# The second mixture's down product in three f32r passes of high and low parts instead of one f32 product

## The reference, cut to what matters

```
logits = xt @ gate_w.T
_, idx = top_k(logits + beta, 2)
c = zeros.at[..., idx].add(sigmoid(logits[idx]))
g = einsum('bh,ehm->bem', xt, gate_proj_w)
u = einsum('bh,ehm->bem', xt, up_proj_w)
h = silu(g) * u
eo = einsum('bem,emh->beh', h, down_proj_w)
combined = einsum('beh,be->bh', eo, c)
... shared_out: the same with the shared weights, without c
x = x + combined + shared_out
```

## Time and profile before

| | |
|---|---|
| median of 3 runs | 2351.04 us (2350.42 to 2353.8) |
| the profiled execution | 2356.89 us |
| its span, first to last instruction | 2355.1 us |
| mean granted TensorE clock over the span | 0.921 |
| TensorE busy | 2025.9 us (86%), weight loads 1358.8 us |
| VectorE, ScalarE, GpSimd busy | 981.7, 1002.4, 674.1 us |
| one expert of the second mixture in the chain | 17.83 us, nine of them |

### The profile page before, as it was taken

The page is one execution under the profiler, slowest core; times in us unless marked ns, Lnnn a source line. Parts: engine busy times, 40 slices in busy tenths (PEclk is TensorE's granted clock), DMA queues, the critical chain, the costliest instruction groups (busy, mean ns, idle before and its releaser), DMA issues. The chain is left out here.

```text
span 2355.1 us, 35383 instructions
## 1 busy us (share of the span) xinstructions
PE 2025.9 (86%) x13548; PEld 1358.8 (58%) x13548; DVE 981.7 (42%) x1616; ACT 1002.4 (43%) x1352; POOL 674.1 (29%) x322
## 2 busy tenths in 40 slices
PE   6599999899978999999998676767898989688899
PEld 2475656656556566665665354436644944356787
DVE  2365454554617545556461244325300700355222
ACT  1144444444434444444443032114798689432321
POOL 1015554454660645445556003001000000000221
PEclk9799999999989999999999588788899989888899
DMA  5200000000021000000000400002454346200121
GB/s 178 61 21 6 5 15 1 15 5 1 1 55 49 6 1 15 5 15 5 1 1 4 121 0 0 1 29 63 75 97 82 76 78 108 73 1 1 54 80 62
DMA packets 81637, 86.43 MB, mean 37 GB/s; under 512 B 29865, under 2 KB 71537, under 8 KB 78161
## 3 DMA queue, kind: packets, MB, share of 16 engines
q1 hardware_dynamic: 74312, 81.35, 14.3%
q10 hardware_dynamic: 7176, 2.94, 0.5%
HBM read 54.38 MB, written 4.72 MB: 25 GB/s over the span
## 5 line engine op out<-in xcount | busy, mean ns | idle before, releaser
L727 POOL TENSOR_TENSOR sums<-sums,probs 128x1024 f32<-128x1024 f32 x224 | 532.9, 2379 | 322.8 <-ACT probs L765 286.8
L819 DVE TENSOR_REDUCE part_max<-psum_banks 128x2 f32<-128x1024 f32 (+1 forms) x256 | 312.1, 1225 | 155.3 <-PE psum_banks L894 151.8
L765 ACT ACTIVATE probs<-psum_banks 128x1024 f32<-128x1024 f32 x240 | 245.9, 1024 | 198.4 <-PE psum_banks L921 194.3
L813 DVE TENSOR_TENSOR keys<-psum_banks,keys 64x512 fp32r<-64x512 f32 x256 | 176.3, 688 | 266.5 <-ACT keys L749 262.1
L932 PE MATMUL psum_banks<-probs,values 128*64 128x256 f32 x2048 | 280.6, 395 | 0.5 <-ACT probs L768 0.5
L2333 ACT ACTIVATE probs<-psum_banks,k_inv_norm 128x1024 f32<-128x1024 f32 x256 | 258.0, 1203 | 3.0 <-PE psum_banks L2348 3.0
L749 ACT ACTIVATE keys<-psum_banks 64x512 fp32r<-64x512 f32 x256 | 151.6, 592 | 223.4 <-PE psum_banks L873 220.3
L910 PE MATMUL psum_banks<-q_hi,keys 128*128 128x256 f32 x1024 | 187.4, 305 | 8.1 <-issue 8.1
L910 PEld LDWEIGHTS psum_banks<-q_hi,keys 128*128 128x128 f32 x1024 | 138.8, 190 | 87.6 <-issue 80.8
L932 PEld LDWEIGHTS psum_banks<-probs,values 128*64 128x64 f32 x2048 | 125.4, 137 | 98.1 <-issue 53.7
L2360 PE MATMUL psum_banks<-probs,values 128*32 128x256 f32 x2048 | 166.7, 398 | 2.3 <-ACT probs L2333 2.3
(11 more groups left out here) (420 smaller groups left out, 3091.5 us busy)
## 6 DMA issues: line engine op xcount, KB each, us to landing
k_pairs<-keys SPq DMA_DIRECT2D x192, 128.0 KB, 4.3
ctx_tok_b<-in_ctx SPq DMA_DIRECT2D x16, 384.0 KB, 4.5
ctx_tok<-in_ctx SPq DMA_DIRECT2D x16, 384.0 KB, 3.5
wk_pair<-wkv_parts SPq DMA_DIRECT2D x16, 256.0 KB, 3.0
wv_quad<-wkv_parts SPq DMA_DIRECT2D x8, 512.0 KB, 3.9
w_gate_up<-in_L_ffn_gate_proj_w SPq DMA_DIRECT2D x8, 512.0 KB, 3.9
w_gate_up<-in_L_ffn_up_proj_w SPq DMA_DIRECT2D x8, 512.0 KB, 4.8
w_down<-in_L_ffn_down_proj_w SPq DMA_DIRECT2D x8, 512.0 KB, 5.6
```

Of the source, the lines that this page charges most:

```text
L727: pool.tensor_tensor(sums[:, :, :, :], probs[:, 0, :, :, :] if step == 1 else sums[:, :, :, :], probs[:, step % SLOTS, :, :, :], ALU.add). ...
L765: act.activation(probs[:, step % SLOTS, :, :, :], scores, ACT.Exp, scale=SCALE0).then_inc(p_ready, 1)
L813: dve.tensor_tensor(keys[rows(1 - h), slot, h, columns_of(c)], psum[rows(h), bank, :], keys[rows(h), slot, h, columns_of(c)].bitcast(F32), ...
L819: dve.tensor_reduce(part_max[:, :, h, c], psum[:, bank:bank + 2, 0:width], AX, ALU.max).then_inc(m_read, 1)
```

## The change

The down product is made like gate and up: three f32r passes per tile and piece, hidden_hi wd_hi, hidden_hi wd_lo and hidden_lo wd_hi. What this adds on the other engines:

- `hidden` shrinks to two buffers that turn with m. Behind each product VectorE waits for ScalarE's copy hidden_hi(m) and subtracts to hidden_lo(m), and TensorE's down(m) waits for hidden_lo(m).
- ScalarE copies hidden_hi(m) in each piece, behind the Silu. Its splitting of the next expert's weights is spread: the wait for the loads and w_hi of gate stand behind Silu(0), w_hi of up behind Silu(1), the new wd_hi behind Silu(2), each ahead of the copy hidden_hi of that piece.
- GpSimd makes wd_lo as a third subtraction. `down_done` starts at four instead of zero, so that ScalarE can wait for the expert before.

The diff, without the new tiles and semaphores:

```diff
                     def down(m):
-                        pe.wait_ge(hidden_ready, e * MT + m + 3)
+                        pe.wait_ge(hidden_lo_ready, e * MT + m + 1)
+                        if m == 0:
+                            pe.wait_ge(wd_lo_ready, e + 1)
                         for t in range(TT):
                             if m == 0:
                                 pe.wait_ge(x_added, e * TT + t + 1)
-                            last = pe.matmul(psum[:, 4 + t, 0:D], hidden[:, m, t * P:(t + 1) * P], wd[:, slot, m, :],
-                                             start=m == 0, stop=m == MT - 1)
+                            for k, (h, w) in enumerate(((hidden_hi, wd_hi), (hidden_hi, wd_lo), (hidden_lo, wd_hi))):
+                                last = pe.matmul(psum[:, 4 + t, 0:D], h[:, m, t * P:(t + 1) * P], w[:, slot, m, :],
+                                                 start=m == 0 and k == 0, stop=m == MT - 1 and k == 2)
...
-                def split(e, slot, lot):
-                    act.wait_ge(arrived[slot], lot * 48 + 48)
-                    for which in range(2):
-                        act.activation(w_hi[:, slot, which, :, :], w_gu[:, slot, which, :, :], ACT.Copy).then_inc(w_hi_ready, 1)
+                def split(slot, lot, part):
+                    if part == 0:
+                        act.wait_ge(arrived[slot], lot * 48 + 48)
+                    if part < 2:
+                        act.activation(w_hi[:, slot, part, :, :], w_gu[:, slot, part, :, :], ACT.Copy).then_inc(w_hi_ready, 1)
+                    if part == 2:
+                        act.activation(wd_hi[:, slot, :, :], wd[:, slot, :, :], ACT.Copy).then_inc(wd_hi_ready, 1)
 
                 def expert(e, slot, lot):
                     for m in range(MT):
                         act.wait_ge(gate_done, e * MT + m + 1)
                         act.wait_ge(hidden_ready, e * MT + m + 1)
                         act.activation(silu[:, m % 2, :], psum[:, m % 2, :], ACT.Silu).then_inc(silu_ready, 1)
-                        if m == 1 and slot is not None:
-
-                            split(e + 1, 1 - slot, lot + slot)
+                        if slot is not None:
+
+                            split(1 - slot, lot + slot, m)
+                        act.wait_ge(hidden_ready, e * MT + m + 3)
+                        if m == 0:
+                            act.wait_ge(down_done, e * TT + TT)
+                        act.activation(hidden_hi[:, m, :], hidden[:, m % 2, :], ACT.Copy).then_inc(hidden_hi_ready, 1)
...
-                        dve.tensor_tensor(hidden[:, m, :], silu[:, m % 2, :], psum[:, 2 + m % 2, :],
+                        dve.tensor_tensor(hidden[:, m % 2, :], silu[:, m % 2, :], psum[:, 2 + m % 2, :],
                                           ALU.mult).then_inc(hidden_ready, 1)
+                        dve.wait_ge(hidden_hi_ready, e * MT + m + 1)
+                        dve.tensor_tensor(hidden_lo[:, m, :], hidden[:, m % 2, :], hidden_hi[:, m, :].bitcast(F32),
+                                          ALU.subtract).then_inc(hidden_lo_ready, 1)
                     for t in range(TT):
-                        dve.wait_ge(down_done, e * TT + t + 1)
+                        dve.wait_ge(down_done, e * TT + t + 1 + TT)
...
+                    pool.wait_ge(wd_hi_ready, e + 1)
+                    pool.tensor_tensor(wd_lo[:, slot, :, :], wd[:, slot, :, :], wd_hi[:, slot, :, :].bitcast(F32),
+                                       ALU.subtract).then_inc(wd_lo_ready, 1)
 
                 split(0, 0)
                 with pool.Fori(0, EX // 2) as i:
                     for slot in range(2):
                         e = i * 2 + slot
                         split(e + 1, 1 - slot)
-                        pool.wait_ge(down_done, e * TT + TT)
+                        pool.wait_ge(down_done, e * TT + 2 * TT)
                         pool.sem_inc(w_free, 1)
```

More of the change, by code:

```diff
@@ L1803, in l1_mixture @@
         silu = core.sbuf(ctx, "silu1", [P, 2, T])
-        hidden = core.sbuf(ctx, "hidden1", [P, MT, T])
+        wd_hi = core.sbuf(ctx, "w_down1_hi", [P, 2, MT, D], F32R)
+        wd_lo = core.sbuf(ctx, "w_down1_lo", [P, 2, MT, D], F32R)
+        hidden = core.sbuf(ctx, "hidden1", [P, 2, T])
+        hidden_hi = core.sbuf(ctx, "hidden1_hi", [P, MT, T], F32R)
+        hidden_lo = core.sbuf(ctx, "hidden1_lo", [P, MT, T], F32R)
         x_hi_ready = core.sem(ctx, "moe1_x_hi")
@@ L1812, in l1_mixture @@
         hidden_ready = core.sem(ctx, "hidden1_ready")
+        hidden_hi_ready = core.sem(ctx, "hidden1_hi_ready")
+        hidden_lo_ready = core.sem(ctx, "hidden1_lo_ready")
+        wd_hi_ready = core.sem(ctx, "moe1_wd_hi")
+        wd_lo_ready = core.sem(ctx, "moe1_wd_lo")
         down_done = core.sem(ctx, "down1_done")
@@ L1881, in expert @@
                         act.activation(silu[:, m % 2, :], psum[:, m % 2, :], ACT.Silu).then_inc(silu_ready, 1)
-                        if m == 1 and slot is not None:
-                            split(e + 1, 1 - slot, lot + slot)
+                        if slot is not None:
[4 more added lines that the diff above has]
+                        act.activation(hidden_hi[:, m, :], hidden[:, m % 2, :], ACT.Copy).then_inc(hidden_hi_ready, 1)
                 act.sem_inc(silu_ready, 2)
+                act.sem_inc(down_done, TT)
                 for c in range(DC):
                     act.activation(x_hi[:, c, :], xnT[:, c, :], ACT.Copy).then_inc(x_hi_ready, 1)
-                split(0, 0, 0)
+                for part in range(3):
+                    split(0, 0, part)
                 with act.Fori(0, EX // 2) as i:
```

## The result

The changed kernel takes 2409.44 us (median of six, 2402.62 to 2414.44), the one before 2352.45 us (six, 2350.42 to 2358.12): a ratio of 1.0237, 95% interval 1.0215 to 1.0258. It is slower by 57 us, where 41.4 were forecast; the time lies above the range of 2379 to 2403. The direction and the place were right, the size was not.

A forecast was written before the change was run, and what follows sets the result against it. The prediction took TensorE's unbroken row of passes to bound the second mixture's nine experts. Seven at +5.95 us and two at -0.15 gave +41.4 us on the median of 2351.04: 2392.4 us, range 2379 to 2403.

The forecast's parts named there:

- The passes, -1.2 us an expert: TensorE's down product: three f32r passes at 0.119 us each replace one f32 product of 0.432 us, 1.2 us less per expert.
- The stall at down(3), 1.05 us in all nine: End of each expert: TensorE waits 1.05 us for the chain of product, copy hidden_hi and subtraction hidden_lo.
- The stall at down(0), 4.35 us in seven experts: Experts 1 to 7: hidden_hi(0) stands behind ScalarE's wait for w_down, so TensorE's first down product stalls 4.35 us.
- hidden_hi(0) 0.62, handover 0.07, subtraction 0.69: Steps in us between the first weight copy, after the w_down load, and TensorE's start of down(0).
- the arrival: When w_down lands for ScalarE in experts 1 to 7: on the mean 7.3 us after the expert's first gate matmul.
- The clock, 1.75 us: TensorE's clock falls in the down(0) stall, costing 1.75 us in each of seven experts; lower bound 0, upper 4.
- The sum: Experts 1 to 7: -1.2 + 1.05 + 4.35 + 1.75 = +5.95 us each; experts 0 and 8: -0.15 each; together +41.4 us.
- the clock that holds: Rival: TensorE's clock holds through the stalls or hardly falls; +29.1 us, 2380 us; chance 0.10.
- the missing stall: Rival: no stall at down(0), only at the expert's end; -1.4 us, 2349.7 us, no measurable change; chance 0.04.
- The rival in which the clock stays low longer: Rival: 4 us lost to TensorE's clock behind each stall; +57 us, 2408 us; chance 0.04.
- Loads that don't overlap: Rival: TensorE weight loads don't overlap matmuls, a pass costs 0.31 us; about 2475 us; chance 0.01.
- the faster side: Rival: TensorE's cheaper passes decide and both waiting chains are covered; saves 10.8 us, 2340.2 us; chance 0.03.

The follow-up runs named there:

- split later: Changed kernel with ScalarE's copy hidden_hi(m) ahead of the split, and the load wait and split parts behind later Silus: 2354.23 us, ratio 1.0008 to the kernel before.
- the filled stall: Changed kernel with 44 useless f32r passes on TensorE ahead of its wait for hidden_lo(0), in every second expert: 2397.97 us, ratio 1.0205 to the kernel before.
- the passes alone: Kernel before with the down product in three f32r passes, weights split, no hidden_lo (high part multiplied again): 2339.32 us against 2350.60, ratio 0.9959.
- the last experiment: Split later with only the hidden_lo passes, put last over all four tiles, waiting for hidden_lo: 2344.84 us, ratio 0.9972 to the kernel before.
- low pass last: Split later with the hidden_hi passes of all four tiles first and only the last four passes waiting for hidden_lo: 2344.84 us, ratio 0.9972.
- GpSimd waiting: Changed kernel with GpSimd waiting for an expert's first hidden_lo before subtracting for the next expert: 2390.85 us, ratio 1.0185 to the kernel before.

## Why the prediction was wrong in size

- **The passes, -1.2 us an expert.** Right: 17.83 - 16.70 = 1.13 measured alone.
- **The stall at down(3), 1.05 us in all nine.** Right. In the chain of the third expert down(2) would end at 2244.28 + 2.76 + 1.43 = 2248.47 and down(3) starts at 2249.26, 0.79 us later; its twelve passes take 1.72 us, 0.29 more than in a row: 1.08 together. The kernel with the split later shows that it eats the gain.
- **The stall at down(0), 4.35 us in seven experts.** Its cause and place were right: the order on ScalarE is what matters, not the load as such, since with the copy ahead of the wait the kernel is 14 us above the one before and not 54. Its size was wrong, at the step "hidden_hi(0) 0.62, handover 0.07, subtraction 0.69". The 0.69 us came from x_lo in the earlier trace rows, a subtraction that ran from 2181.93 on, while GpSimd was still idle (it starts at 2183.45). Here it took 2.43 us, and 0.69 once GpSimd was held back. That term was short by 1.74 us, 12.2 for seven, and it is the failed step. A smaller slip went the other way: the arrival was counted from the first gate matmul's record, 2225.63, but the 5.45 us of passes start at 2225.98 in the chain, 0.35 us later, so that without GpSimd the stall is 4.0, not 4.35. 4.0 + 1.74 = 5.7, as measured.
- **The clock, 1.75 us.** The fall was right, and the filled stall shows the cause. What stands behind the stall took 2.28 us more, between the taken value and the upper bound of 4; over seven experts that is 3.7 us beyond the forecast. Some 0.23 of the 2.28 are there at the full clock too (1.66 against 1.43), a restart behind a wait that the sum had no term for.
- **The sum.** 5.95 + 1.74 - 0.35 + 0.53 = 7.9 us an expert against 8.02 measured; the passes (1.13 for 1.2) and the stall at down(3) (1.08 for 1.05) are most of the rest. The range had no room for the subtraction, because I treated a duration from a row as fixed; I had asked which engines wait for each other, not which run at the same time.

The rivals: the clock that holds and the missing stall are refuted. The rival in which the clock stays low longer, 4 us lost each, gave 2408 us, next to the measured 2409.44, but by luck: what it lost to the clock was 2.28 us, and the subtraction that it left at 0.69 made up for the rest. Loads that don't overlap are refuted by the passes alone, and the faster side is real only if the two waits go, as the last experiment does in part.

The Trainium skill has the rule that would have warned of this. The Trainium skill's page "SBUF — State Buffer", section "🔬 SBUF: two separate sides", says that VectorE and GpSimd share a pair of SBUF ports as an exclusive lock, taken for a whole instruction, by a VectorE operation with two SBUF inputs against a GpSimd operation that reads SBUF. The trace agrees: the product hidden, with one operand in PSUM, takes 0.69 us beside GpSimd as ever, while hidden_lo with two in SBUF lasts 2.42 us. That is waiting, not half speed, and the other subtractions of the same expert tell the two apart. This is hidden_lo(1):

```profile
2236.99 1.49 DVE L1932 TENSOR_TENSOR hidden_lo<-hidden,hidden_hi 128x512 fp32r<-128x512 f32 x1 [0.70 <-ACT hidden_hi L1902]
```

When it starts, GpSimd has 0.94 us left (2232.80 + 5.13 = 2237.93), and it takes 1.49. hidden_lo(2) starts at 2244.34 with 1.16 us of GpSimd's w_down_lo left (2243.10 + 2.40 = 2245.50) and takes 1.70. hidden_lo(0) starts with some 1.90 left (2.38 - 0.48) and takes 2.42. Each takes what GpSimd has left and 0.52 to 0.55 us more. At half speed beside GpSimd, an estimate from these numbers, hidden_lo(1) would have taken 0.69 + 0.94 / 2 = 1.16 us and hidden_lo(2) 0.69 + 1.16 / 2 = 1.27.

## What to carry to other kernels

When an edit puts a new instruction behind a wait on an in-order engine, list what else is queued behind it; the price is the arrival time, not the length of the instruction. Then take each new duration at the time at which it will run, and ask which engine is active beside it: here the moved split put GpSimd's work exactly beside the subtraction that TensorE waited for. And where an operand comes in a quick and a slow part, let the passes that need only the quick one go first.

## What the runs showed of the hardware that was not expected

- A VectorE subtraction of two SBUF tiles (128x512) took 0.69 us alone, and up to 2.55 us beside a GpSimd subtraction of 2.38 us: what GpSimd had left when it started, and about 0.55 us more. GpSimd suffers less: 2.87 us at most for one (split later, low pass last), and 5.13 to 5.22 us for two where the pairs of the kernel before took 4.64 to 4.75.
- Idle gaps of TensorE of 1.56 us left the granted clock at 1.00; those of 3.7 to 4.3 us (GpSimd waiting) and of 5.6 to 6.1 us (the changed kernel) were each followed by a stretch at half speed, and the longer ones did not cost clearly more, 2.28 us on the mean against 2.16. Useless matmuls in the gap kept it at 1.00 and gave 2.2 us an expert.
- The same kernel's executions differ by up to 20 us (2342 to 2362 us in the 37 of the one before that ran beside the experiments), and the trace of the changed kernel gained 9 us in stages that the change doesn't touch. Within the loop, traces agree to 0.1 us where the clock is full.
